# Layer 0's combining: no clearing between gathers, and a wait for landed rows at every second token tile

## The reference, cut to what matters

```
x = x + 0.5 * ffn(layernorm(x))
x = x + attention(layernorm(x))
x = x + 0.5 * ffn(layernorm(x))

ffn(x):  top-4 of 32 experts per token;  y[token] += expert(x[token]) * weight   for its 4 experts
         z = (silu(x @ Ws1) * (x @ Ws3)) @ Ws2                                   shared expert, all tokens
         return y + z
attention: qkv = x @ qkv_w.T + qkv_b;  softmax(q k / 4) v;  @ proj_w.T + proj_b
```

## Time and profile before

| | |
|---|---|
| median of 3 runs | 3122.12 us (3119.54 to 3123.11) |
| the profiled execution's own time | 3125.94 us |
| its span, first to last instruction | 3124.2 us |
| mean granted clock of TensorE | 0.951 of full speed |
| busy share of the span | PE 88%, DVE 66%, ACT 73%, POOL 25% |
| routing and experts, layer 0 | until 420 us |
| layer 0's combining and projections | 423 to 682 us |
| attention | from 696 us on |
| layer 1's combining | 2928 us to the end |

### The profile page before, as it was taken

The page is one execution under the profiler, slowest core; times in us unless marked ns, Lnnn a source line. Parts: engine busy times, 40 slices in busy tenths (PEclk is TensorE's granted clock), DMA queues, the critical chain, the costliest instruction groups (busy, mean ns, idle before and its releaser), DMA issues. The chain is left out here.

```text
span 3124.2 us, 60171 instructions
## 1 busy us (share of the span) xinstructions
PE 2747.6 (88%) x16841; PEld 1088.5 (35%) x16844; DVE 2068.7 (66%) x3847; ACT 2276.9 (73%) x3449; POOL 789.1 (25%) x1158
## 2 busy tenths in 40 slices
PE   5599987869999999999999999999999775999854
PEld 5388744432222212222212222212111162887422
DVE  5744446656868768687776877868778667444344
ACT  2644423449999999999999999999999725444200
POOL 5455557621000000000000000000000044555577
PEclk9999989989999999999999999999999885999966
DMA  5555554430001001010010010010000035555633
GB/s 158 151 155 156 146 114 113 120 83 12 3 3 26 3 11 18 3 25 3 5 24 3 5 24 5 3 24 5 3 4 3 31 102 170 155 156 145 116 107 111
DMA packets 132051, 195.30 MB, mean 63 GB/s; under 512 B 22364, under 2 KB 99324, under 8 KB 130428
## 3 DMA queue, kind: packets, MB, share of 16 engines
q1 hardware_dynamic: 104188, 117.00, 13.3%
q0 software_dynamic: 27648, 75.53, 10.1%
HBM read 124.85 MB, written 67.50 MB: 62 GB/s over the span
## 5 line engine op out<-in xcount | busy, mean ns | idle before, releaser
L1640 ACT ACTIVATE RB<-psS 128x1024 f32<-128x1024 f32 x1920 | 1766.2, 1213 | 8.5 <-PE psS L1558 8.3
L1592 PE MATMUL psO<-RB,values 128*32 128x512 f32 x7680 | 1025.9, 606 | 0.5 <-ACT RB L1640 0.5
L1558 PE MATMUL psS<-WE 51*128 51x512 f16 x3840 | 695.3, 387 | 80.2 <-POOL values L1497 11.2
L1558 PEld LDWEIGHTS psS<-WE 51*128 51x128 f16 x3840 | 174.3, 93 | 1093.5 <-ACT RB L1640 1071.4
L638 POOL DMA_INDIRECT xg<-xn_d,index x320 | 304.8, 953 | 228.9 <-issue 197.6
L662 PE MATMUL psH<-WE,xgt 128*128 x1280 | 341.7, 390 | 2.2 <-DVE xgt L706 2.2
L1511 POOL COPY values<-WE 128x512 f32 x12 | 7.0, 611 | 1319.2 <-PE psO L1592 1319.2
L726 ACT ACTIVATE gate<-psH 128x128 f32<-128x128 f32 x320 | 88.7, 277 | 249.0 <-PE psH L662 241.8
L711 DVE TENSOR_TENSOR hid<-gate,psH 128x128 f32<-128x128 f32 x320 | 92.1, 288 | 258.2 <-ACT gate L726 225.5
L1656 DVE TENSOR_SCALAR part<-psO 128x512 f32<-128x512 f32 x256 | 172.0, 672 | 114.8 <-PE psO L1558 114.7
L1592 PEld LDWEIGHTS psO<-RB,values 128*32 128x32 f32 x7680 | 151.3, 108 | 277.1 <-issue 245.3
(11 more groups left out here) (245 smaller groups left out, 3249.4 us busy)
## 6 DMA issues: line engine op xcount, KB each, us to landing
pair_d<-ob SPq DMA_DIRECT2D x320, 128.0 KB
WE<-part_d SPq DMA_DIRECT2D x84, 128.0 KB
xn_d<-ws SPq DMA_DIRECT2D x64, 128.0 KB, 1.7
WE<-in_W SPq DMA_DIRECT2D x2, 4096.0 KB, 23.4
part_d<-raw SPq DMA_DIRECT2D x32, 256.0 KB
xg<-xn_d,index POOLq DMA_INDIRECT x320
RA<-in_x SPq DMA_DIRECT2D x8, 512.0 KB, 7.6
head_d<-sums SPq DMA_DIRECT2D x128, 32.0 KB, 1.6
```

What stands on the lines that cost most here:

```text
L1558: return pe.matmul(ps, K[r][rows, kt * P:(kt + 1) * P], Q[r][rows, at:at + BLK], start=True, stop=True)
L1592: last = pe.matmul(psO[g % 2][32 * j:32 * (j + 1), :], values[:, r, j % 2, kt, :], weights, start=(kt == 0), stop=(kt == KT - 1))
L1640: act.activation(probs[n % RING][:, half * 2 * BLK:(half + 1) * 2 * BLK], psS[m % HELD][:, :], ACT.Exp, scale=SCALE).then_inc(sem("exped"), 1)
```

## The change

In layer 0's combining GpSimd's clearing after each gather goes, with its semaphore. In its place, at tiles 2, 4, 6, ..., 30, GpSimd waits for the four gathers of the tile before to have landed. Since the gathers of earlier tiles had to land before DVE could use them, or are waited for at the even tile before, no gather is under way when such a wait ends.

```diff
@@ combine_project
-    pause = spare[:, YS * D:YS * D + P]
@@ block.gpsimd
                 for t in range(NT):
                     pool.wait_ge(f_sem("y_used"), (t + 1) * TOPK)
+                    if t >= 2 and t % 2 == 0:
+                        for k in range(TOPK):
+                            pool.wait_ge(y_in[(t - 1) % AHEAD * TOPK + k], (t - 1) // AHEAD * 16 + 16)
                     carried(pool, f_sem("seen_pool"))
                     for k in range(TOPK):
                         s = t % AHEAD * TOPK + k
                         pool.indirect_dma_start(Y[:, s, :], None, pair_d,
                                                 bass.IndirectOffsetOnAxis(ap=pair_slot[:, t, k:k + 1], axis=0))\
                             .then_inc(y_in[s], 16)
-                        if t * TOPK + k >= 1:
-                            pool.wait_ge(f_sem("paused"), t * TOPK + k)
-                        pool.memset(pause[:, 0:P], 0.0).then_inc(f_sem("paused"), 1)
```

## The result

The kernel after took 3104.45 us (median of 7 runs, 3100.27 to 3110.55), the kernel before 3119.65 (7 runs, 3114.87 to 3126.56): ratio 0.9952 with an interval of 0.9937 to 0.9966, 15.2 us faster where I forecast 8. The profiled execution of the kernel after took 3100.27 us, with a span of 3098.6.

The account below looks back on a forecast made before the run. No engine was full after 482 us in layer 0's combining; TensorE's semaphores reached ACT late while gathers ran. Gains of 7 + 1 = 8 us gave 3118 from the profiled 3125.94, or 3114 as median; 8-in-10 range 3096 to 3136.

Parts of the forecast that it names:

- Clearings, direct worth 0: Layer 0's combining: removing GpSimd's 128 clearings gains 0 on the path, since only the next clearing waits for one.
- late words: TensorE's semaphores reaching ACT up to 14 us late in layer 0's combining; 48.7 us of ACT's waits from 481 to 638 us.
- A wait makes a moment with no gather under way: Layer 0's combining: landing waits give moments without gathers, letting TensorE's backlog of delayed semaphores clear; 8 us off.
- the first episode: TensorE's delayed semaphores to ACT, cleared at 505.69 us; clearing 2.8 to 6 or up to 12 us earlier, taken as 7.
- the four later ones: Delays in the second tile pair of later four-tile blocks, ending with its last landing; four times 0.3, 1 us gained.
- Does DVE notice? Cost 0: Layer 0's combining: the feed slows by 0.5 to 1.45 us per pair, but DVE's rows still land in time; at worst 1.45 us once.
- remote: Profile's name for waits on a semaphore that comes with no instruction just ended to explain it; ACT's are always for TensorE.
- C: Rival: the clearings delay TensorE in layer 0's combining; all delays go, 35 us, 3087; chance 0.17 including gains short of it.
- a landing of 2.3 us: The Trainium skill's estimate for a 128 KB gather: a pair takes 0.4 us less, its landing wait almost free.
- A: Rival: denser gathers in layer 0's combining make TensorE's semaphores later, 17 to 40 us less what waits clear; 3142, chance 0.20.
- B: Rival: nothing happens; the delays belong to TensorE's own work or the free moments miss them; 0, 3122 us, chance 0.20.
- D: Rival: the wait starves DVE of rows at tiles 6 to 8 if a landing takes 6 us; 3126 us, chance 0.03.

Follow-up runs that it names:

- the second chip: The kernels before and after, both unchanged, run again on another chip against before at 3059.22 us: before 3059.07 us, after 3082.16 us (1.0076).

## Why the prediction was right, and which step failed

**Clearings, direct worth 0: right.** Without them the ratios were 0.9999 and 0.9996 where no late words exist (both intervals hold 1), and a clearing of one column changes nothing. The step came down to 1.25 us, the upper of my two bounds.

**A wait makes a moment with no gather under way, which clears the words: right, and mis-sized.** I gave 7 us to the first episode and 1 to the four later ones together, since the later ones "end with its last landing, which stays their first free moment". The backlog forms less where the free moments come every 12.4 to 14.2 us: nearly all late words went (ACT's from 52.1 us to 6.1), and with them the episodes that I had left in place. Had nothing else changed, that would have given up to the 42.4 us by which the stage is shorter where no late words exist.

**"Does DVE notice? Cost 0": this step failed.** It rested on "every tile from 8 on is wanted more than 6 us after it would land". That distance was read from a trace in which DVE was itself held up by the late words: 27.64 us for a block, 13.8 for a pair. The same edit removed the delay, and with it the cover. The closest place, tile 7, was read at that pace too. Nothing was late from 450 to 482 us, as the forecast says, but something had been just ahead of it: ACT has 3.4 us of "remote" waits that end at 446 and 447 us, and DVE's first adding stood at 450.39 us, after at 443.52. So the kernel after reached tile 7's last row at 474.67 and not at 480.4, and waited 0.77 us for it. What the block needs without late words is 22.7 us, 11.35 a pair. My own two numbers for the new feed, 11.3 and 12.25 us, should have been held against that pace; one stood already in the argument for C, 22.18 us near the end of the stage. At 1.25 us a step the waits then cost 0.9 us a pair at the least and 13.5 us over 15 pairs. Measured were 12.4 to 14.2 a pair, as the wait takes 3.6 to 4.9 us from gather to gather and not 3.5 (on the second chip 2.7 to 4.0 to the landing and 0.91 to the restart, where I took 2.7 and 0.8), and 23 us in all. The forecast also says that with a landing of 2.3 us the wait would be almost free. That holds at 1.12 us a step alone: at 1.25 a pair would still take 11.85 us, more than 11.35. And the landings measured are longer, 2.8 us in the median of the 128.

**The sum, as the runs show it:** 42.4 us of late words gone, less 23.4 for the emptied queue (the stage of after less that of before on the second chip), is 19; the stages of the comparison differ by 20.4, the medians by 15.2. My 8 was the difference of two terms that were both too small. That they fell on the right side together is luck in part: on three of the five chips of the experiments the edit has nothing to clear.

**The rivals.** *A* was wrong for this change and has the sign for its first half: clearings away without waits costs 16 us on one chip, and layer 0's stage is longer on both chips with late words that ran it (266.8 and 271.6 us) than in the comparison's profile of before (253.9). The sum of the late words is less clear: 52.9 and 61.5 us for ACT against 52.1, 29.8 and 28.9 for DVE against 18.3. *B* holds on no chip: the change is 15 us faster or 23 slower. *C* falls: all clearings gone, late words longer. *D* had the mechanism (DVE waits for rows), with 3.3 us at tiles 7 and 8 where it is the whole stage. Its condition was put too high: it asked for a landing of 6 us, and one of 2.7 was enough, since the pace that the feed must hold is 11.35.

**What stays open.** Why words of TensorE come late in some runs and not in others, and by what way a gather under way holds them up. That the waits clear them is shown, by three numbers of waits and in two layers. That it is the free moment, and not the slower feed that comes with it (12.4 us and more a pair against 10.8), rests on the times at which the longest waits end. The runs don't separate the two: the wait for older rows, which has no free moment and no slower feed, met no late words, and a slower feed without a free moment was not tried.

The recording itself is a rival that nothing here rules out. The five profiles with late words lack a third of the records of semaphore updates: they hold 23,613 to 24,939, the nine others 34,973 to 35,242 (of the 2048 by layer 0's gathers 417 to 651, and 2039 to 2045). Every run of the record has a span and a clock, so it was recorded in some way. Whether words come late without recording isn't known, nor so what the change is worth there.

Nor is it shown that the clearings hold words back by spacing the gathers: a spacing without GpSimd work was not tried. The version without any clearings or waits in either layer (0.9960) was run only where no words are late; as its part in layer 0 costs 16 us where they are, it is no answer for all chips.

## What to carry to other kernels

Slack that is read from a trace is slack at that trace's pace: when an edit removes the delay that made it, hold the new feed against the pace without the delay, here 12.4 us a pair against 11.35. A wait that leaves nothing under way costs a whole landing each time (3.7 us instead of a step of 1.25), one for work a tile older cost nothing where no words are late. And run an edit on more than one chip before it is kept, when what it cures shows as "remote".

## What the runs showed of the hardware

- **The same program differs by 2% from chip to chip.** Before took 3058.0, 3059.2 and 3058.9 us on the first three chips, and 3119.7, 3115.7 and 3117.9 in the comparison and on the fourth and fifth. No chip shows both times (up to 27 runs each); none of the five was used twice, so the chip isn't told apart from the time of its runs, nor from the way in which they were recorded. Of the 63.7 us between the spans of before's two profiles 42 lie in layer 0's combining, 13 in the gathers' stretch of layer 1's (170.9 and 183.9), where indirect gathers run beside TensorE. None of the nine profiles from the first three chips has a "remote" wait of ACT or DVE from 423 to 700 us.
- **The same change has two signs:** 0.9952 with late words, 1.0076 without. Half as many waits: 0.9971 and 1.0017, so 10.5 us won for 5.6 lost.
- **A small GpSimd instruction fits into the gap between two gathers.** A clearing of 128 x 1 took 0.12 us and left the step at 1.25 us; one of 128 x 128 took 0.22 and made it 1.34:

```profile
503.12 0.95 POOL L1014 DMA_INDIRECT WE<-pair_d,pair_slot  x1 [0.16 <-issue]
504.07 0.11 POOL L1019 MEMSET WE<- 128x1 f32 x1
504.37 0.95 POOL L1014 DMA_INDIRECT WE<-pair_d,pair_slot  x1 [0.19 <-issue]
```
